# Edge products of a graph layer: one fp32 product per tile, or two fp32r products of rows that VectorE weights

## The reference

```python
support = X @ W                                   # X = layernorm(x), 12500 x 256
msgs = support[edge_src] * edge_val[:, None]
out = jax.ops.segment_sum(msgs, edge_dst, num_segments=N_NODES)
x = x + out + b
# then: y = layernorm(x); route all rows to the 2 best of 8 experts (256 -> 512 -> 256, exact gelu),
# chosen from the mean row; out = layernorm(y_experts + y, gamma, beta); x = x + out
```

## Time and profile before

| | |
|---|---|
| median of 3 runs | 2383.69 us (2382.87 to 2384.53) |
| the profiled execution | 2382.08 us, its span 2380.3 us |
| PE busy | 2210.0 us (93%) |
| POOL busy | 1516.3 us (64%) |
| ACT busy | 1193.3 us (50%) |
| DVE busy | 1025.3 us (43%) |
| DMA | 425.79 MB, mean 179 GB/s |
| granted TensorE clock | 0.985 of full speed |

### The profile page before, as it was taken

The page is one execution under the profiler, slowest core; times in us unless marked ns, Lnnn a source line. Parts: engine busy times, 40 slices in busy tenths (PEclk is TensorE's granted clock), DMA queues, the critical chain, the costliest instruction groups (busy, mean ns, idle before and its releaser), DMA issues. The chain is left out here.

```text
span 2380.3 us, 41661 instructions
## 1 busy us (share of the span) xinstructions
PE 2210.0 (93%) x9949; PEld 1729.8 (73%) x9950; DVE 1025.3 (43%) x2952; ACT 1193.3 (50%) x3202; POOL 1516.3 (64%) x1594
## 2 busy tenths in 40 slices
PE   2488999899999999999999999999998999999998
PEld 1366777677776767777777777777776777999998
DVE  7893233232332233232332322232222235899989
ACT  3577666665655555544534343322324125565664
POOL 6777777777777777777777777777777771000100
PEclk9999999999999999999999999999999999999999
DMA  9955667666666655566656656556566554242431
GB/s 369 336 168 157 205 202 241 187 189 180 180 187 181 181 176 175 178 179 197 186 178 180 189 179 187 175 182 190 169 194 172 186 161 141 95 140 95 136 98 54
DMA packets 226740, 425.79 MB, mean 179 GB/s; under 512 B 36675, under 2 KB 134774, under 8 KB 226600
## 3 DMA queue, kind: packets, MB, share of 16 engines
q0 software_dynamic: 75008, 204.90, 29.5%
q1 hardware_dynamic: 151160, 217.12, 28.0%
q10 hardware_dynamic: 432, 2.40, 0.3%
HBM read 341.53 MB, written 82.75 MB: 178 GB/s over the span
## 5 line engine op out<-in xcount | busy, mean ns | idle before, releaser
L588 POOL DMA_INDIRECT G<-xr_d,SRC x1467 | 1391.8, 949 | 447.0 <-issue 298.6
L1072 DVE TENSOR_SCALAR OH<-CST,DL,WR 128x128 f32<-128x128 f32 x1563 | 567.4, 370 | 1272.3 <-PE ps L1463 1151.0
L1463 PE MATMUL ps<-G,OH 128*128 x3126 | 739.8, 389 | 78.6 <-DVE OH L1072 57.8
L1463 PEld LDWEIGHTS ps<-G,OH 128*128 128x128 f32 x3126 | 597.0, 194 | 224.1 <-issue 143.0
L1446 PE MATMUL ps<-W2u,H 128*128 128x256 f32 x1920 | 430.9, 382 | 6.9 <-issue 6.3
L1435 PE MATMUL ps<-YU,W1u 128*128 128x512 f32 (+1 forms) x1024 | 426.1, 568 | 9.6 <-ACT H L767 8.4
L1446 PEld LDWEIGHTS ps<-W2u,H 128*128 128x128 f32 x1920 | 363.1, 191 | 69.8 <-issue 20.9
L1435 PEld LDWEIGHTS ps<-YU,W1u 128*128 128x128 f32 x1024 | 194.8, 191 | 206.1 <-issue 184.7
L775 ACT ACTIVATE YE<-ps 128x512 f32<-128x512 f32 (+1 forms) x128 | 72.6, 569 | 442.3 <-PE ps L1446 442.1
L767 ACT ACTIVATE H<-ps,b1a 128x512 f32<-128x512 f32 (+1 forms) x256 | 168.5, 660 | 225.9 <-PE ps L1435 225.6
L602 POOL TENSOR_TENSOR ZR<-ZV,mhalf 128x4 f32<-128x4 f32 (+1 forms) x24 | 30.5, 1272 | 348.6 <-DVE ZV L1256 348.6
(11 more groups left out here) (221 smaller groups left out, 2302.1 us busy)
## 6 DMA issues: line engine op xcount, KB each, us to landing
W1u<-in_W SPq DMA_DIRECT2D x64, 512.0 KB
W2u<-in_W SPq DMA_DIRECT2D x64, 512.0 KB, 4.7
y_d<-YE SPq DMA_DIRECT2D x56, 512.0 KB, 5.7
G<-xr_d,SRC POOLq DMA_INDIRECT x1467
x_d<-X SPq DMA_DIRECT2D x98, 128.0 KB
yt_d<-YT SPq DMA_DIRECT2D x98, 128.0 KB
XR<-in_x SPq DMA_DIRECT2D x97, 128.0 KB, 3.1
XL<-x_d SPq DMA_DIRECT2D x24, 512.0 KB, 4.9
```

The costliest lines, as they stand in the source:

```text
L588: e.indirect_dma_start(out=G[0:rows(s), held(s), :], out_offset=None, in_=x if s < FRESH else xr_d, in_offset=bass.IndirectOffsetOnAxis(ap ...
L1072: e.tensor_scalar(OH[:, s % OHR, :], iota, DL[:, s:s + 1], WR[:, s + 1:s + 2], ALU.is_equal, ALU.mult).then_inc(s_oh, 1)
L1463: e.matmul(ps[:, 0, 0:D], OH[:, r, :], Gf[:, bass.ds(g + r * D, D)], start=False, stop=True, skip_group_check=True).then_inc(s_main, 1)
```

## The change

Tiles from 96 on: DVE no longer puts the weight into the one-hot. It makes unweighted one-hots for four tiles in one operation (`one_hots`, 128 x 512), and for each tile two operations on the gathered rows: the high part (rows times weight, rounded to fp32r) and the low part (rows times weight, less the high part), both into the new ring `GW` of 16 places. TensorE multiplies the same one-hot with both, two fp32r products. The first 96 tiles are weighted too (`weighted`, one operation a tile, float32) but keep the one fp32 product. As the weighted rows are a copy, a place of `G` comes free when DVE has done the low part; `G` has 36 places in place of 72, `OH` 16 in place of 8, GpSimd waits for places and for landings only at every fourth tile, and DVE waits for landings of four tiles together. `OHX` needs no weight, so that ScalarE's two scaled copies per node tile are gone. In the last 44 tiles 28 places of `G` are in use; the last three tiles are weighted one by one (`last_parts`).

```diff
-RING, GS, OHR = 64, 16, 8
+HELD, GS, LOT, RING = 36, 9, 4, 16
+OWN, TURN = 8, NE - 44
 FRESH, XBUF = 96, 18
-HELD = RING + OHR
 def held(s):
-    return s if s < OHR else OHR + (s - OHR) % RING
+    return s % HELD if s < TURN else OWN + (s - TURN) % (HELD - OWN)
+
+def before(s):
+    return s - (HELD if s < TURN + HELD - OWN else HELD - OWN)
...
             for s in range(NE):
-                if s >= HELD:
-                    e.wait_ge(s_main, s - RING + 3)
-                if s == inner:
-                    for l in sorted({lot_of[k] for k in INNER}):
-                        e.wait_ge(xs_st[l], 16 * LOTS[l])
-                if s >= GS:
-                    e.wait_ge(gat[s % GS], 16 * (s // GS))
+                if s >= HELD and s % LOT == 0:
+                    e.wait_ge(s_gw, before(s) + LOT)
+                if s >= GS * LOT and s % LOT == 0:
+                    e.wait_ge(gat[s // LOT % GS], 16 * LOT * (s // (LOT * GS)))
...
             def copy(v, t):
-                e.load([thr_r], THR[0:1, t:t + 1])
-                odd = e.snap(thr_r, min_val=1, max_val=NE - 1)
-                e.wait_ge(s_main, odd + 1)
-                if t:
-                    e.wait_ge(s_begin, t)
-                e.wait_ge(s_act, chain)
-                for k in range(2):
-                    e.activation(OHX[:, k, :], OHT[:, 1, k, :], ACT.Copy, scale=WR[:, bass.ds(odd + k, 1)]).then_inc(s_ohx, 1)
...
-            def one_hot(s):
-                if s < FRESH:
-                    e.wait_ge(s_pow, STEPS * (batch_of[s] + 1))
-                elif rows(s):
-                    e.wait_ge(gat[s % GS], 16 * (s // GS + 1))
+            def one_hots(s, m):
                 if s == 0:
                     e.wait_ge(s_tab, tab_dl)
-                if s >= OHR:
-                    e.wait_ge(s_main, s - OHR + 1)
-                e.tensor_scalar(OH[:, s % OHR, :], iota, DL[:, s:s + 1], WR[:, s + 1:s + 2], ALU.is_equal, ALU.mult).then_inc(s_oh, 1)
+                if s >= RING:
+                    e.wait_ge(s_main, s - RING + m + 1)
+                e.tensor_tensor(out=OH[:, s % RING:s % RING + m, :], in0=iota.unsqueeze(1).to_broadcast([P, m, P]),
+                                in1=DL[:, s:s + m].unsqueeze(2).to_broadcast([P, m, P]), op=ALU.is_equal).then_inc(s_oh, m)
+
+            def weighted(s):
+                if s % LOT == 0:
+                    one_hots(s, LOT)
...
+                e.wait_ge(s_pow, STEPS * (batch_of[s] + 1))
+                if s % LOT == 0:
+                    e.wait_ge(s_oh, s + LOT)
+                e.tensor_scalar(GF[:, s % RING, 0, :], G[:, held(s), :], WR[:, s + 1:s + 2], None, ALU.mult).then_inc(s_gw, 1)
+
+            def parts(s):
+                one_hots(s, LOT)
+                e.wait_ge(gat[s // LOT % GS], 16 * LOT * (s // (LOT * GS) + 1))
+                for j in range(s, s + LOT):
+                    e.tensor_scalar(GW[:, j % RING, 0, :], G[:, held(j), :], WR[:, j + 1:j + 2], None, ALU.mult).then_inc(s_gh, 1)
+                e.wait_ge(s_oh, s + LOT)
+                for j in range(s, s + LOT):
+                    e.wait_ge(s_gh, j - FRESH + 1)
+                    e.scalar_tensor_tensor(out=GW[:, j % RING, 1, :], in0=G[:, held(j), :], scalar=WR[:, j + 1:j + 2], in1=GW[:, j % RING, 0, :].bitcast(f32), op0=ALU.mult, op1=ALU.subtract).then_inc(s_gw, 1)
...
-            def edge(g, r):
-                e.matmul(ps[:, 0, 0:D], OH[:, r, :], Gf[:, bass.ds(g + r * D, D)], start=False, stop=True, skip_group_check=True).then_inc(s_main, 1)
...
+            def edge(r, fresh):
+                if fresh:
+                    ins = e.matmul(ps[:, 0, 0:D], OH[:, r, :].bitcast(f32), GF[:, r, 0, :], start=False, stop=True, skip_group_check=True)
+                else:
+                    for h in range(2):
+                        ins = e.matmul(ps[:, 0, 0:D], OH[:, r, :], GW[:, r, h, :], start=False, stop=True, skip_group_check=True)
+                ins.then_inc(s_main, 1)
```

More of the change, by code:

```diff
@@ L110 @@
 assert 2 * NEV <= 512
-assert NE % OHR == 4 and EDGES <= (NE - 1) * P
+assert NE % RING == 12 and FRESH % RING == 0 and EDGES <= (NE - 1) * P
+assert TURN % HELD == OWN and all(held(s) == held(before(s)) for s in range(HELD, NE))
 def gnn_ffn(nc, x, dflat, srct, dstt, wt, W, b, Wr, br, W1, b1t, W2, b2, gamma, beta, cst, iota_e, evt, out):
@@ L313, in gnn_ffn @@
         EARLY = sum(between)
[L314 removed]
+        assert EARLY <= RING + 4
         nf = FULL // P
@@ L1104, in _ @@
                 newton_steps(FRESH // 8 - 1, range(4 * j, 4 * j + 4))
-                one_hot(FRESH - 12 + j)
-            for s in range(FRESH - 8, NE - 1):
-                one_hot(s)
+                weighted(FRESH - 12 + j)
+            for s in range(FRESH - 8, FRESH):
+                weighted(s)
+            for s in range(FRESH, NE - LOT, LOT):
+                parts(s)
+            for s in range(NE - LOT, NE - 1):
+                last_parts(s)
             rn = 0
@@ L1420, in chores, with begin @@
                 ins.then_inc(s_tr, 1)
-            def begin(v, g):
-                e.wait_ge(s_ohx, v * 2)
+            def begin(v, r, fresh):
+                e.wait_ge(s_ohx, v)
                 e.wait_ge(s_as, v + 1)
-                e.matmul(ps[:, 0, 0:D], OHX[:, 0, :], Gf[:, bass.ds(g, D)], start=True, stop=False, skip_group_check=True)
-                e.matmul(ps[:, 0, 0:D], OHX[:, 1, :], Gf[:, bass.ds(g + D, D)], start=False, stop=True, skip_group_check=True).then_inc(s_begin, 1)
+                for k in range(2):
+                    if fresh:
+                        ins = e.matmul(ps[:, 0, 0:D], OHX[:, k, :].bitcast(f32), GF[:, r - 1 + k, 0, :], start=(k == 0), stop=(k == 1), skip_group_check=True)
+                    else:
+                        for h in range(2):
+                            ins = e.matmul(ps[:, 0, 0:D], OHX[:, k, :], GW[:, r - 1 + k, h, :], start=(k == 0 and h == 0), stop=(k == 1 and h == 1), skip_group_check=True)
+                ins.then_inc(s_begin, 1)
             def unit_up(u, m):
@@ L1455, in by_size @@
                     do(u, GT)
-            v_r, u_r, ev_r, due, kind, now_r, rel, lap_r = (e.alloc_register(n) for n in ("section", "unit", "event", "due", "kind", "now", "ahead", "lap"))
-            for r_ in (v_r, u_r, ev_r, lap_r):
+            v_r, u_r, ev_r, due, kind, now_r, rel = (e.alloc_register(n) for n in ("section", "unit", "event", "due", "kind", "now", "ahead"))
+            for r_ in (v_r, u_r, ev_r):
                 e.reg_mov(r_, 0)
             e.load([due, kind], EVT[0:1, 0:2])
-            def edge(g, r):
-                e.matmul(ps[:, 0, 0:D], OH[:, r, :], Gf[:, bass.ds(g + r * D, D)], start=False, stop=True, skip_group_check=True).then_inc(s_main, 1)
+            def edge(r, fresh):
+                if fresh:
+                    ins = e.matmul(ps[:, 0, 0:D], OH[:, r, :].bitcast(f32), GF[:, r, 0, :], start=False, stop=True, skip_group_check=True)
+                else:
+                    for h in range(2):
+                        ins = e.matmul(ps[:, 0, 0:D], OH[:, r, :], GW[:, r, h, :], start=False, stop=True, skip_group_check=True)
+                ins.then_inc(s_main, 1)
             def following(a):
@@ L1487, in event, with slots @@
                         with e.If(now == END):
-                            begin(e.snap(v_r, min_val=1, max_val=FINAL), g + (r - 1) * D)
-            def slots(a, g, n):
-                for r in range(n):
-                    if r % 4 == 0:
-                        e.wait_ge(s_oh, a + (r + 4))
-                    edge(g, r)
-                    if r % 2 == 1:
-                        event(a, r, g)
-            with e.Fori(0, NE // OHR) as i:
-                a = e.snap(i * OHR)
-                g = e.snap(lap_r, min_val=0, max_val=RING * D)
-                e.reg_mov(rel, e.snap(due) - a)
-                slots(a, g, OHR)
-                e.reg_mov(lap_r, (e.snap(lap_r, min_val=0, max_val=RING * D) & (RING * D - 1)) + OHR * D)
+                            begin(e.snap(v_r, min_val=1, max_val=FINAL), r, fresh)
+            def slots(first, last, fresh):
+                with e.Fori(first // RING, last // RING) as i:
+                    a = e.snap(i * RING)
+                    e.reg_mov(rel, e.snap(due) - a)
+                    for r in range(RING):
+                        if r % LOT == 0:
+                            e.wait_ge(s_gw, a + (r + LOT))
+                        edge(r, fresh)
+                        if r % 2 == 1:
+                            event(a, r, fresh)
+            slots(0, FRESH, True)
+            slots(FRESH, NE // RING * RING, False)
             def last_across():
```

70 lines of the change are left out of this document (45 added, 25 removed).

## The result

The changed kernel takes 4016.26 us (median of 3 runs, 4004.87 to 4022.36) where the kernel before took 2383.69: 1.6841 times as long, 95% interval 1.6781 to 1.6902. The profiled execution has a span of 4003.1 us at a mean granted TensorE clock of 0.743. The prediction, 2488 us in a range of 2418 to 2558, is far off. Its sign was right, but most of the 1633 us that were added have a cause that it did not consider.

What follows compares the result with a forecast made beforehand. GpSimd's gathers, 1.25 us a tile, were taken to bound the kernel. On the profiled 2382.1 us: +29.5 (stall), +0.5 (square-root lots), +73 (disturbed gathers), +1.3 (end) = 2486.4, or 2488 on the median; range 2418 to 2558.

Steps and rivals of the forecast that it cites:

- What bounds the kernel now: Edge stage: GpSimd's gathers set the end at 1.25 us a tile; TensorE's pace decides nothing beyond some 3 us.
- The GpSimd stream covers all of it: TensorE waits instead.: Edge products: the 286 us of TensorE time saved by cheaper products is hidden behind the gathers and gains nothing.
- the rival in which TensorE sets the pace: Edge stage: cheaper products shorten GpSimd's 0.30 us gap; with a gap of 0.2, 2268 us; chance 0.03.
- The smaller ring and the stall: Gathered rows, 36 places for 72: GpSimd stops at tile 36, gather 44 starts 32.6 us late, net +29.5 us.
- Waits on GpSimd at nothing: GpSimd's gathers: three of four lose their wait instructions, but the gap is 0.30 us without waits too, so 0.
- What DVE does to GpSimd: Gathers wait out DVE operations with two SBUF inputs: 0.05 us a gather, +73 us; upper bound 0.11, 160 us.
- The prediction's sum by that rule: Gathers beside DVE: only the high parts disturb them, 0.006 us a gather, 9 us in all, sum 2422.
- DVE's work per tile: DVE in the edge stage: from 370 to 1001 ns a tile, about 0.87 us in runs, under 1.25, no bound.
- Edge products at 0.24 us a tile: TensorE's edge stage: two fp32r products take 0.24 us a tile, 0.195 less than one fp32 product.
- The end: Behind the last gather: +0.3 us for the last tile's work and 1 for a slower second-stage start, +1.3.

Runs made afterwards that it cites:

- e13: Changed kernel with rings of 12 places instead of 16, so 12 tiles a pass: 2620.97 us beside 2384.06, ratio 1.0998.
- e9: Kernel before with one added DVE subtraction (two SBUF inputs) for each of tiles 104 to 399, into scratch: 2394.09 us beside 2384.82.
- e16: Kernel before with the same added subtractions as e9, but issued four in a row at every fourth tile: 2414.44 us.
- e7: Changed kernel with TensorE's main loop split at tile 400, the second loop without code for small units: 2879.88 us, ratio 1.2059.
- e4: Kernel before with two groups of 8 tiles in one pass of TensorE's edge loop: 4407.02 us beside 3225.38, ratio 1.3653.
- e15: e13's kernel with DVE's high and low parts of each four tiles mixed instead of four highs, then four lows: 2686.33 us.
- e8: Kernel before with one added DVE multiply (one SBUF input) for each of tiles 104 to 399, into scratch: 2386.55 us beside 2384.82.
- e3: Kernel before with 1152 never-run instructions behind a false condition in TensorE's loop body: 3243.06 us, ratio 1.0051.
- e14: e13's kernel with one-hots made by four operations of one SBUF input instead of one with two: 2627.66 us beside 2620.97.

## Why the prediction was wrong, step by step

**What bounds the kernel now: right for before.** Where no code is fetched GpSimd sets the end: e13's last gather is explained to within 2 us by the stall and the gathers' lengths, and e9 and e16 moved the end (9 and 30 us) by what they did to the gathers (0.030 and 0.102 us for each of 296).

**The failed step: "The GpSimd stream covers all of it: TensorE waits instead."** It priced TensorE by its products and looked at nothing else that 16 tiles a pass bring; the sum has no term for the instructions themselves and so puts them at nothing without a reason, and the rival in which TensorE sets the pace was only considered on the fast side. The row of the instruction queue stands on the page of the kernel before (27 packets in all), and the loop went from 8 to 16 tiles with the same code a tile. The price: 4016.26 - 2620.97 = 1395 us between the changed kernel and e13's, for 839 - 34 = 805 blocks, 1.73 us a block, the slower clock (0.743 against 0.893) included. The two differ in four ring places too, but e7 keeps 16, and e4 shows the effect without the change.

**The smaller ring and the stall: right.** Forecast: gather 36 at 86.2 and gather 44 at 100.9, +29.5 us. Measured 84.47 and 100.04 (e13: 84.35, 99.95, and +28.6). DVE reached the first one-hots at 82.28 us, 1.9 sooner than the prediction's "no sooner than" 84.15, and the work up to tile 44 took longer than it had put, so that a part of the nearness at tile 44 is luck.

**Waits on GpSimd at nothing: right.** The gap is 0.30 us with and without waits (441.9 us over 1450 gaps in e13).

**What DVE does to GpSimd: right in kind, mis-sized.** Forecast +73 us, 0.05 us a gather, upper bound 0.11; measured 0.139 and 204 us in e13 with rings of 12, and 0.108 in e7 with rings of 16 once the fetches stop, which would be 158 us over 1467 gathers. The formula took each operation as a hold of its own; e16 and e15 show holds through a whole run of operations. That the moments are not random either, since DVE starts a lot when a gather lands, was not tested. For the changed kernel's own trace the term reads 1006 - 949 = 57 ns, nearly as forecast, but there GpSimd mostly stood still, so this agreement proves nothing. By what the Trainium skill's page "SBUF — State Buffer", section "Who interferes with whom", infers of descriptor generation, a multiply that runs in a two-port mode should stall GpSimd and an operation with two SBUF inputs should not: e8 and e9 show the reverse, gathers of 950 and 978 ns beside 948. The measurement decides. (The prediction's sum by that rule, 2422, stands on the profiled execution; on the median, like its 2488, it is 2424.)

**DVE's work per tile: right.** Forecast 1001 ns; e13's groups give 681/4 + 374 + 472 = 1016, and DVE is no bound.

**Edge products at 0.24 us a tile: near.** In e13 a run of twenty products takes 2.95 us, 0.28 to 0.30 us a tile, at a granted clock near 0.9.

**The end: small.** +1.3 forecast, +3.0 in e13.

Put together, the forecast for the edits without the fetches is 2488 where e13 has 2621, outside the range too, by 63 us. No run has 16 places and no fetches throughout; with e7's 0.108 us a gather the same sum gives an estimate of 2384 + 28.6 + 158 + 3.0 = 2573 us, still outside by 15, and 1443/805 = 1.79 us a block. No version here beats the kernel before on chips where it takes 2384: the edits lengthen the one stream that sets its end.

## What to carry to other kernels

When a change makes a loop's body longer, count the instructions of a pass on each engine and read the instruction queues' rows of the page; when a pass touches more blocks than stay in the store it pays for its code again each time, here 1.7 to 1.8 us for each 256 instructions. It pays most where few of the 256 are run: a block came in about every 3.2 us, and where its code kept TensorE busy for longer (19 us in the second stage) the fetch was hidden. Code that was skipped in whole blocks (1152 instructions in e3) was not fetched and cost 0.5%, so rarely used paths can be laid outside, while paths that are interleaved with the hot code (as the small units here) count in full. Beside a stream of GpSimd gathers, DVE operations with two SBUF inputs are dear when they stand in unbroken runs: spread, one subtraction a tile cost 0.03 us a tile; four in a row cost 0.10 (30 us over 296 tiles).

## What the runs showed of the hardware that was not expected

- TensorE's store keeps the blocks of a loop of 1033 instructions, and of one of about 1540, over all passes (27 and 34 blocks in all), and at 2048 or 2070 it keeps next to none: 8.4 and about 10 blocks are fetched in each pass. Where between 1540 and 2048 it turns was not tried.
- A jump over 1152 instructions, 195 times, fetched no block and cost at most 0.7% (ratio 1.0051, at most 1.0074). By the Trainium skill, page "Runtime: NRT & Kernel Launch", section "Instruction fetch mechanics", a taken branch out of a window of two pages forces a fetch; the loops of 1033, 1366 (e7) and about 1540 instructions jump back over as many, and after their first pass no fetch is seen in them.
- On three of the five chips of the experiments the kernel before took 3225 to 3262 us with all its instructions the same; TensorE's semaphore updates came late and in bunches. A kernel that is bound elsewhere (the changed one) lost 0.6% there.
- A gather that was held ends 0.80 to 0.85 us after the end of the operation, or of the run of operations, that held it (446 of 451 in e13). The longest here took 3.19 us for 0.95 (e14); it began among the multiplies and ended 0.9 us after the last of the four subtractions behind them, so that in a run the operations of one SBUF input seem to hold too.
- A block of 256 instructions costs TensorE nothing where its code runs long enough: 21 blocks in the second stage of the changed kernel, with no idle time on TensorE between 3650 and 3990 us.
